# Nine products of the second attention's first query tile before the parts' border, query weights split before context

## The reference, cut to what matters

```python
x = x + _L0_xattn_ref(_layernorm(x), ctx_4096, ...)
x = x + _L0_ffn_ref(_layernorm(x), c1_w, c2_w, w1, w2t)
x = x + _L1_xattn_ref(_layernorm(x), ctx_4096, mask, Wq, Wk, Wv, Wo, q_norm_w, k_norm_w)
x = x + _L1_ffn_ref(_layernorm(x), weight, bias, centroids, assignments)

# the sparse feed-forward part
h = relu(einsum('bkm,bm->bk', w1[idx], xf))
out = einsum('bk,bkm->bm', h, w2t[idx])
# the second attention: 32 query heads in 8 groups that share keys and values, 128 wide
q = (hidden @ Wq.T)          # rms norm per head
k = (context @ Wk.T); v = (context @ Wv.T)
out = softmax(q k^T * scale + mask) v @ Wo.T
```

## Time and profile before

| | |
|---|---|
| median of 3 runs | 1483.95 us (1482.55 to 1486.05) |
| the profiled execution's own time | 1484.29 us |
| its span in the trace | 1482.5 us |
| TensorE (PE) matmul busy | 1455.0 us, 98% |
| weight loads (PEld), beside the matmuls | 851.0 us, 57% |
| VectorE (DVE), ScalarE (ACT), GpSimd (POOL) | 75%, 54%, 48% |
| mean granted TensorE clock | 0.999 of full speed |
| share of the chain that ended last by engine | PE 59%, DVE 3%, ACT 2%, POOL 1% |

### The profile page before, as it was taken

One profiled execution on the slowest core, in us unless ns is written; L12 is line 12 of the kernel. 1 busy time (PEld: TensorE's weight loads), 2 busy tenths in 40 slices (PEclk: granted clock), 3 DMA queues, 4 the chain that ended last, 5 costly groups with the idle time before them and its releaser, 6 DMA issues.

```text
span 1482.5 us, 27790 instructions
## 1 busy us (share of the span) xinstructions
PE 1455.0 (98%) x9944; PEld 851.0 (57%) x9944; DVE 1118.6 (75%) x2159; ACT 793.5 (54%) x3201; POOL 714.0 (48%) x672
## 2 busy tenths in 40 slices
PE   8999999999999989999999999999999999999998
PEld 6888745555555455556555555655555565556554
DVE  5887787878876878676776776776676677677867
ACT  5678741211222775565646645654754665565663
POOL 6668885454556354343334424333443434343554
PEclk9999999999999999999999999999999999999999
DMA  6744435344344585534543543444344345333543
GB/s 192 219 170 139 125 88 122 99 80 107 65 81 71 122 164 92 129 89 72 104 93 61 105 78 82 94 93 83 86 89 97 79 79 110 55 61 68 104 72 127
DMA packets 363722, 150.04 MB, mean 101 GB/s; under 512 B 346704, under 2 KB 347344, under 8 KB 360640
## 3 DMA queue, kind: packets, MB, share of 16 engines
q1 hardware_dynamic: 362288, 140.92, 44.6%
q10 hardware_dynamic: 1296, 7.34, 1.5%
HBM read 60.11 MB, written 4.19 MB: 43 GB/s over the span
## 4 chain that ended last, share of the span: by engine, by line
PE 59%; DVE 3%; ACT 2%; POOL 1%; SPq 1%; DMA 1%; issue 0%; POOLq 0%; ACTq 0%; DVEq 0%
PE bank L72 19%; PE bank L74 18%; PE bank L73 18%; PE bank L2672 3%; ACT a_prob L1989 1%; DVE x_res L2348 0%; DMA a_kT_lo<-a_kn_lo 0%; DVE a_oT_lo L2261 0%; ACT xln L124 0%; POOL a_xr_lo L1863 0%; DVE a_kn L2216 0%; SPq L1735 0%; DVE a_qve L2200 0%; DVE a_p_lo L2249 0%; SPq L1717 0%
## 5 line engine op out<-in xcount | busy, mean ns | idle before, releaser
L1989 ACT ACTIVATE a_prob<-a_prob,a_nmx 128x64 f32<-128x64 f32 x512 | 170.2, 334 | 247.8 <-DVE a_nmx L2237 247.8
L1838 POOL TENSOR_TENSOR a_prob<-a_prob,a_mask 128x512 f32<-128x512 f32 x64 | 79.9, 1270 | 271.8 <-DVE a_prob L2231 271.8
L72 PE MATMUL bank<-w,xT_hi 128*128 128x448 f16 (+1 forms) x512 | 187.5, 366 | 1.1 <-PEq L1043 1.1
L74 PE MATMUL bank<-w,xT_hi 128*128 128x448 f16 (+1 forms) x512 | 187.3, 366 | 0.0
L73 PE MATMUL bank<-w,xT_lo 128*128 128x448 f16 (+1 forms) x512 | 187.2, 366 | 0.0
L1856 POOL TENSOR_TENSOR a_qrs<-a_qve,neg_half 128x8 f32<-128x8 f32 x64 | 104.9, 1641 | 137.9 <-DVE a_qve L2200 137.6
L2184 DVE SCALAR_TENSOR_TENSOR x_res<-bank,a_oinv,x_res 128x512 f32<-128x512 f32 x128 | 95.4, 746 | 79.5 <-PE bank L74 79.5
L1251 ACT CAST f_h_hi<-h 128x448 f16<-128x448 f32 x64 | 35.6, 563 | 207.3 <-DVE h L1325 207.2
L2189 DVE SCALAR_TENSOR_TENSOR a_qr_lo<-bank,a_qr_hi 128x512 f16<-128x512 f32 x128 | 87.9, 687 | 46.2 <-ACT a_oT_lo L1966 27.3
L1844 POOL TENSOR_TENSOR a_p_hi<-a_prob,a_rden 128x512 f16<-128x512 f32 x64 | 69.5, 1087 | 104.9 <-DVE a_rden L2245 104.9
L1189 POOL TENSOR_TENSOR f_h_lo<-h,f_h_hi 128x448 f16<-128x448 f32 x64 | 72.7, 1140 | 89.0 <-ACT f_h_hi L1251 89.0
(11 more groups left out here) (357 smaller groups left out, 4440.2 us busy)
## 6 DMA issues: line engine op xcount, KB each, us to landing
shared<-in_l_wq SPq DMA_DIRECT2D x8, 1024.0 KB, 5.0
shared<-in_l_wo SPq DMA_DIRECT2D x8, 1024.0 KB, 5.4
shared<-in_w ACTq DMA_DIRECT2D x8, 896.0 KB, 4.5
craw<-in_w SPq DMA_DIRECT2D x11, 512.0 KB, 4.0
a_wide<-in_l_ctxT SPq DMA_DIRECT2D x16, 256.0 KB, 3.9
x_res<-in_x SPq DMA_DIRECT2D x16, 256.0 KB, 4.4
shared<-in_ctx SPq DMA_DIRECT2D x16, 256.0 KB, 4.3
shared<-in_l_wkv SPq DMA_DIRECT2D x8, 512.0 KB, 3.6
```

The lines of the kernel that those rows point to most:

```text
L72: pe.matmul(out, a_hi, b_hi, start=first, stop=False)
L74: return pe.matmul(out, a_hi, b_lo, start=False, stop=last)
L1838: pool.tensor_tensor(blocks(prob[u][:, :]), blocks(prob[u][:, :]), mask[:, :].unsqueeze(1).broadcast_to([P, NB, S]), ALU.add).then_inc(s_m ...
L1989: ins = act.activation(pt, pt, ACT.Exp, bias=nmx[:, col:col + 1], accum_out=den[:, col:col + 1])
```

## The change

Four edits. On ScalarE the four `wq_hi` pieces go ahead of `cT0_hi`. On VectorE the four `wq_lo` pieces and `add_out(14)` go ahead of `cT0_lo`. On TensorE, in the first part, three waits and four matmuls of query tile 0 (steps k = 0 and 1, the two of each that need only `wq_hi`) are put between `out_half(14, 1)` and `out_half(15, 0)`, and behind `out_half(15, 1)` a wait for `wql_ok` and the other five matmuls of steps 0 to 2. In the second part the first query then computes step k = 3 alone (three matmuls). No matmul is added or dropped, and the bank is `bank[2]` both times.

```diff
@@ ScalarE, end of the first part
             ins.then_inc(m.wkvh_ok, 1)
-            act.activation(m.cT0_hi, r.c, ACT.Copy, scale=m.wscale[:, 4:5]).then_inc(m.s_cTh, 1)
             for k in range(KD):
                 act.activation(m.wq_hi[:, k, :], r.q[:, k, :], ACT.Copy, scale=m.wscale[:, 0:1]).then_inc(m.wqh_ok, 1)
+            act.activation(m.cT0_hi, r.c, ACT.Copy, scale=m.wscale[:, 4:5]).then_inc(m.s_cTh, 1)
@@ VectorE, end of the first part
             ins.then_inc(m.wkvl_ok, 1)
-            dve.wait_ge(m.s_cTh, 1)
-            dve.scalar_tensor_tensor(m.cT0_lo, r.c, m.wscale[:, 4:5], m.cT0_hi, ALU.mult, ALU.subtract).then_inc(m.s_cTl, 1)
-            add_out(NT - 2)
             for k in range(KD):
                 dve.wait_ge(m.wqh_ok, k + 1)
                 ins = dve.scalar_tensor_tensor(m.wq_lo[:, k, :], r.q[:, k, :], m.wscale[:, 0:1], m.wq_hi[:, k, :], ALU.mult,
                                                ALU.subtract)
             ins.then_inc(m.wql_ok, 1)
+            add_out(NT - 2)
+            dve.wait_ge(m.s_cTh, 1)
+            dve.scalar_tensor_tensor(m.cT0_lo, r.c, m.wscale[:, 4:5], m.cT0_hi, ALU.mult, ALU.subtract).then_inc(m.s_cTl, 1)
             add_out(NT - 1)
@@ TensorE, end of the first part
             out_half(n - 1, 1)
+
+            l1_rows, l1_query = slice(0, P), bank[2]
+            pe.wait_ge(s_hm, NT * NQ - 2)
+            pe.wait_ge(s_xT, 32 * (4 * TPC + 1))
+            pe.wait_ge(m.wqh_ok, 2)
+            for k in range(2):
+                pe.matmul(l1_query[:, :], m.xT_hi[:, k, l1_rows], m.wq_hi[:, k, :], start=k == 0, stop=False)
+                pe.matmul(l1_query[:, :], m.xT_lo[:, k, l1_rows], m.wq_hi[:, k, :], start=False, stop=False)
             out_half(n, 0)
             out_half(n, 1)
+            pe.wait_ge(m.wql_ok, 1)
+            for k in range(2):
+                pe.matmul(l1_query[:, :], m.xT_hi[:, k, l1_rows], m.wq_lo[:, k, :], start=False, stop=False)
+            split_mm(pe, l1_query[:, :], m.xT_hi[:, 2, l1_rows], m.xT_lo[:, 2, l1_rows], m.wq_hi[:, 2, :], m.wq_lo[:, 2, :],
+                     False, False)
             pe.wait_ge(s_xT, 32 * len(passes) * TPC)
@@ TensorE, start of the second part
-            query(0, 0, 0, 0, first=True)
+            query_waits(0, 0, 0, first=True)
+            query_part(0, 0, range(3, KD)).then_inc(s_q, 1)
             query(0, 0, 1, 0, first=True)
```

## The result

| | before | after |
|---|---|---|
| median of 22 runs each, same chip | 1483.93 us (1481.39 to 1486.38) | 1487.82 us (1483.62 to 1488.83) |
| ratio to before, 95% interval | | 1.0025, [1.0019, 1.0031] |
| span of the profiled execution | 1482.5 us | 1486.4 us |
| its mean granted TensorE clock | 0.999 | 0.996 |

The kernel became 0.25% slower, 3.7 us by the ratio. The forecast was 1486.2 us with a range of 1484.0 to 1489.6, so the time is inside it, but in part by luck: the range was that wide because of the rival with the falling clock, and the clock did fall. The forecast's own range, without that rival, ended at 1487.8. The shift of 3.7 us is 1.5 more than the 2.2 that was forecast.

What follows compares the result with a forecast made beforehand. TensorE was taken as the bound, without a gap from 600 to 1369 us. It comes 1.87 us late past query tile 0, 2.2 us through the queues; 1483.95 + 2.2 = 1486.2 us, range 1484.0 to 1489.6.

Steps and rivals of the forecast that it cites:

- the rival with the falling clock: TensorE's clock falls to 1.2 GHz behind the standstill, adding 3.2 us on the path, to 1489.4 us; chance 0.14.
- The forecast's own range: Total time without the rivals: 1484.8 to 1487.8 us, from the parts' bounds and the spread of medians; chance 0.68.
- The standstill: Ahead of out_half(15, 0): TensorE waits for two wq_hi pieces from 480.17 to 483.65 us, 3.48 us.
- parts one to three: From the early wait through query tile 0: border 3.81 us later, TensorE 1.87 us late at the tile's last matmul.
- The border's own cost: At the border, from TensorE's last matmul end to its next start: 0.31 us, against 1.12 before.
- the low parts: Ahead of the five matmuls before the border: wq_lo is done at 486.5 us, wanted at 493.6, so no wait.
- stayed at 1.00: Claim that after standstills of up to 1.5 us ahead of the border the TensorE clock kept its full rate.
- the shorter gaps cost nothing: Argument against the falling clock: TensorE works without a gap around the standstill, and shorter gaps had no price.
- The queues: Behind the border: other queues start 3.81 us late; SP's delay moves kT and scores(0, 0) by 2.57 us.
- Part four: Behind the border: VectorE's first score tile starts 2.15 us late; TensorE takes over 2.2 us and keeps it.
- The delay was not absorbed: Answers the rival that 1.9 us vanish in TensorE's waits between 492 and 540 us, about 1484.3 us; chance 0.09.
- the rival without a standstill: Ahead of out_half(15, 0): weights ready at 480.2 us, SP queue allows only 0.4 us gain, 1483.55 us; chance 0.05.

Runs made afterwards that it cites:

- the kernel with work in the standstill: Changed kernel plus 15 matmuls of no use ahead of the early waits; ratio to before 1.0027, on another chip 1.0037.
- the variant between the halves: Changed kernel with its early waits and four early matmuls moved between out_half(15, 0) and out_half(15, 1); ratio to before 0.9994, second look 0.9990.
- four alone: Against before, only the four wq_hi matmuls moved, between out_half(15, 0) and out_half(15, 1), the other eight behind the border; ratio 0.9999.
- between, late: The variant between the halves plus nine matmuls of no use ahead of the border; ratio to before 1.0003.

## Why the prediction was right and wrong

**The standstill: right.** 3.48 us forecast, 3.50 measured, released by `wq_hi` as said. The kernel with work in it confirms the whole of parts one to three: border +3.79 against +3.81, TensorE +1.85 against +1.87. The border's own cost, 0.31 forecast, is 0.30; the gap between the last halves is gone; the low parts were in time (L1573 follows without a gap).

**The clock: a term put at nothing that was not nothing.** The forecast kept the clock at 2.4 GHz in its sum and gave its fall a chance of 0.14. It fell in both profiles of the changed kernel, and only 5 of 33 executions have a mean of 1.000. The sentence that failed is that the clock "stayed at 1.00" after the gaps of 1.5 us: rows 2 begin at 478 us and say nothing of them. The trace of before, asked there, has a fall of its own, first in TensorE's timeline and then in the busy times by stretch:

```profile
42.36 0.66 PE L913 MATMUL bank<-ident,a_wide 128*128 128x128 f32 x4 [1.46 <-DVE a_wide L696]
42.85 0.34 PE L969 MATMUL bank<-ident,a_prob 128*128 128x128 f32 x1
42.88 0.74 PE L72 MATMUL bank<-a_big 128*128 128x512 f32 x1
43.41 0.63 PE L73 MATMUL bank<-a_big 128*128 128x512 f32 x1
```

```profile
42.00:43.00 1.00, 0.64 (x6) 0.65 (x7) 1.00 (x3) 0.25 (x1) 0.62 (x1) 0.96 1.53 316
43.00:44.00 1.00, 1.00 (x5) 0.81 (x4) 0.97 (x3) 0.95 (x3) 0.86 (x2) 0.50 1.25 106
```

A gap of 1.46 us there was followed by half clock, and the mean of 0.999 on the page was the hint. The same gap stands in all 14 profiles, and in twelve of them the clock stayed up behind it, as in the variant between the halves, TensorE's timeline and the busy times by stretch:

```profile
41.51 0.66 PE L913 MATMUL bank<-ident,a_wide 128*128 128x128 f32 x4 [1.44 <-DVE a_wide L696]
```

```profile
42.00:43.00 1.00, 1.00 (x7) 0.87 (x6) 0.97 (x4) 0.80 (x3) 0.86 (x2) 1.00 1.55 124
```

So the row of before would not have made the fall certain. It takes away the ground of "the shorter gaps cost nothing", and with it that of the 0.14. The rival's price, 3.2 us, was too high: the slow matmuls are 7, not some 15, and cost 1.4 us where they stand. On this the Trainium skill, "TensorE: Matmul & The Clock Gate", section "Why this matters for your kernels", which warns of long idle gaps between bursts, agrees with the traces at 2.88, 3.50 and 5.39 us. The falls behind gaps near 1.4 us go beyond that warning, and there the traces decide. The forecast set rows against it that didn't cover the question.

**The queues: mechanism right, the last step wrong.** That everyone else starts with the border and that SP has the least slack is what happened. The step to the issue of `kT` was also right: forecast 1.24 us less than the border's shift, measured 1.25 less in the changed kernel (+3.96 for +5.21). The gap of 1.4 us that was forecast ahead of `scores(0, 0)` came as two, 0.83 there and 0.56 ahead of `scores(0, 1)`. What failed is the step behind it. Part four went on with VectorE's first score tile, 1.66 less than the border, and made that TensorE's delay. But `scores(0, 1)` can't start before the query tiles that are issued behind the keys on the same queue, and so the queue's delay, 1.0 to 1.3 less than the border, holds. For the border that was forecast it means 2.6 instead of 2.2 us; in the kernel with work in the standstill it was 3.2, where the transposes of `qT_lo` took 3.58 us instead of 2.6 in the first profile and 3.4 in the second.

**The sum** from the common zero: 1.87 (TensorE at full clock) + 1.42 (seven slow matmuls) + 0.8 (queues) makes 4.1, measured 4.04 at the first attend. Near the end it is 4.45 and 4.09, by the ratio of times 3.7 and 4.1. The forecast was 2.2: it lacked the 1.42 and had 0.3 in place of the 0.8. That this is all of the difference is shown for the first attend, not for the end, where the five executions of mean clock 1.000 are 3.1 us slower than those of before without any fall.

**The other rivals.** The delay was not absorbed: between 497 and 545 us TensorE idles 5.6 us in after, against 4.8 in before. And the rival without a standstill, 1483.55 us by the old median, which is 0.4 us under before, was run as the variant between the halves: border and TensorE came out as worked out (+0.3, -1.64), but the SP queue let more through than the 0.4 us that the rival allowed, 0.9 to 1.0 at the first attend. The gain is 0.5 to 1.2 us in the traces behind that, and 0.9 to 1.5 in the time.

**A faster version.** The variants that move eight or nine with four of them between the halves are the fastest by the ratios. Two of their three intervals lie just under 1 (0.9991, [0.9982, 0.9999], and 0.9990, [0.9981, 0.9999]), the third does not (0.9994, [0.9985, 1.0002]). All nine behind the last half, 0.9995, can't be told from them, nor can four alone, 0.9999. A gain of about 1 us, 0.07%, is likely and near what can be told at all.

**What stays open.** How much of the clock's 1.4 us reaches the end. Changed kernel against the one with work in the standstill says 0 to 0.8. The two falls at 541 us (between, late, and the first profile with work in the standstill) say little too: they put 1.4 and 1.7 us on the shift between 540 and 545 us, but at the last matmul it stands only 0.5 and 0.8 above its value at 540, where the profiles without that fall move by -0.2 to +0.6. On the other side, executions of before with a mean clock of 0.999 or 0.998 are 1.7 to 2.2 us longer than those with 1.000. Nor is it shown why the kernels with added matmuls met longer transposes of `qT_lo`.

## What to carry to other kernels

When a step is moved ahead in a queue that is the bound, ask first when its inputs are there, and put it behind the work that can run until then: the same nine matmuls cost 3.7 us in one place and gave some 1 us, if anything, one half product later. A hole that already exists (0.81 us ahead of the last half) is the place for it. And moving work of one engine across a point where all meet makes every other queue later by what was moved; that is free only up to the slack of the tightest of them, here 1.0 to 1.3 us in the queue of DMA issues.

## What the runs showed of the hardware

The granted TensorE clock fell to 1.2 GHz behind each standstill of 2.88, 3.50 (two profiles) and 5.39 us. It also fell behind much shorter ones, but in some profiles only, though the same gap stands in all 14: behind 1.36 to 1.37 us near 167 us in five, behind 1.44 to 1.46 us near 42 us in two (one is that of before), behind 1.9 to 2.3 us near 539 us in two. A long standstill doesn't bring a fall in every execution either: of the kernels with one of 2.88 us or more 6 of 46 executions have a mean clock of 1.000, so no fall (that they have the same standstill is taken from their profiles, not seen); of before 33 of 81, of the variants without a standstill 35 of 87. The stay at the lower level was longer behind the longest, 11 matmuls of 512 columns against 7, in the one profile that has it. Executions of one and the same kernel differ by up to 6 us (before: 1481.0 to 1486.9), and the start of the same instruction by 3.4 us between profiles, without any of it coming from the change. The meeting of all engines at the border costs 0.30 us from TensorE's last matmul to its next in all variants in which TensorE comes last, and 1.12 us where VectorE has a 0.75 us instruction behind it.
